# Blank matrix products and an early one-column gelu in the last image's back half

## What is computed

```python
out = softmax(q k^T * scale + rel_h + rel_w) @ v      # per window and head
x = shortcut + out @ proj_w + proj_b
y = layer_norm(x) * ln2_g + ln2_b
y = gelu(y @ fc1_w + fc1_b)                           # 192 -> 768, exact gelu
return x + (y @ fc2_w + fc2_b)                        # 768 -> 192
```

## Time and profile before

| | us |
|---|---|
| median of 3 runs | 534.57 |
| lowest, highest | 530.46, 537.25 |
| the profiled execution's own time | 535.51 |
| its span, first to last instruction | 533.7 |
| mean granted TensorE clock over the span | 0.965 |

### The profile page before, as it was taken

One profiled execution on the slowest core, in us unless ns is written; L12 is line 12 of the kernel. 1 busy time (PEld: TensorE's weight loads), 2 busy tenths in 40 slices (PEclk: granted clock), 3 DMA queues, 4 the chain that ended last, 5 costly groups with the idle time before them and its releaser, 6 DMA issues.

```text
span 533.7 us, 12298 instructions
## 1 busy us (share of the span) xinstructions
PE 508.3 (95%) x4544; PEld 463.4 (87%) x4544; DVE 390.2 (73%) x924; ACT 265.4 (50%) x526; POOL 135.9 (25%) x318
## 2 busy tenths in 40 slices
PE   7999889999999999999999999999999999998947
PEld 7999768899998999999998989999989899776737
DVE  5237887879888888879888888888887978764130
ACT  2112434565555565635545555646555555555602
POOL 1213222323122423223132324232232323220110
PEclk9669898999999999999999999999999999999978
DMA  6962232342404040401304040404031221303000
GB/s 170 250 164 76 68 105 86 98 120 58 133 16 143 2 143 3 134 12 52 93 17 129 2 144 2 142 3 129 16 111 34 74 72 33 113 2 93 0 16 15
DMA packets 29760, 40.98 MB, mean 77 GB/s; under 512 B 5796, under 2 KB 14468, under 8 KB 29700
## 3 DMA queue, kind: packets, MB, share of 16 engines
q1 hardware_dynamic: 29699, 40.20, 26.2%
HBM read 6.57 MB, written 1.57 MB: 15 GB/s over the span
## 4 chain that ended last, share of the span: by engine, by line
PE 89%; DVE 4%; issue 3%; ACT 3%; POOL 1%; DMA 0%; DVEq 0%; POOLq 0%; ACTq 0%
PE back L1250 17%; PE back L1469 12%; PE by_key L1409 9%; PE times_v L1419 9%; PE by_query L1394 9%; PE front_b L1250 8%; PE front_b L1362 6%; PE front_a L1362 6%; PE front_a L1250 4%; PE back L1435 2%; PE by_key L1286 2%; PE back L1442 1%; PE back L1298 1%; PE front_a L1298 1%; PE front_a L1371 1%
## 5 line engine op out<-in xcount | busy, mean ns | idle before, releaser
L1189 DVE TENSOR_REDUCE row_max<-by_query 128x2 f32<-128x512 f32 x186 | 127.7, 687 | 44.6 <-PE by_query L1394 43.4
L959 ACT ACTIVATE probs<-by_key 128x512 f32<-128x512 f32 x192 | 110.4, 596 | 76.6 <-PE by_key L1409 71.7
L1394 PE MATMUL by_query<-k_stack,q_stack 108*128 108x256 f32 x372 | 80.5, 298 | 2.4 <-DVE row_max L1189 2.3
L1409 PE MATMUL by_key<-q_stack,k_stack 110*128 110x256 f32 x384 | 80.4, 306 | 2.3 <-ACT probs L959 2.3
L1469 PE MATMUL back<-w,hid 128*128 128x192 f32 x384 | 69.6, 326 | 0.0
L1394 PEld LDWEIGHTS by_query<-k_stack,q_stack 108*128 108x128 f32 x372 | 57.5, 191 | 10.1 <-issue 6.6
L1409 PEld LDWEIGHTS by_key<-q_stack,k_stack 110*128 110x128 f32 x384 | 56.9, 190 | 10.3 <-issue 6.2
L1469 PEld LDWEIGHTS back<-w,hid 128*128 128x128 f32 x384 | 61.5, 190 | 0.3
L1250 PE MATMUL back<-xn_hi,w_hi 128*128 128x256 f32 x192 | 53.6, 290 | 1.9 <-DVE xn_hi L1098 1.6
L1250 PE MATMUL back<-xn_hi,w_lo 128*128 128x256 f32 x192 | 53.0, 287 | 0.0
L1419 PE MATMUL times_v<-probs,v_ones 128*32 128x256 f32 x768 | 52.3, 390 | 0.0
(11 more groups left out here) (138 smaller groups left out, 1000.2 us busy)
## 6 DMA issues: line engine op xcount, KB each, us to landing
q_stack<-q_hi SPq DMA_DIRECT2D x32, 192.0 KB, 2.7
k_stack<-k_hi SPq DMA_DIRECT2D x32, 192.0 KB, 3.1
q_stack<-rel_hi SPq DMA_DIRECT2D x32, 168.0 KB
q_stack<-rel_lo SPq DMA_DIRECT2D x32, 168.0 KB
q_stack<-q_lo SPq DMA_DIRECT2D x16, 192.0 KB, 3.0
k_stack<-k_lo SPq DMA_DIRECT2D x16, 192.0 KB, 3.1
X<-in_x SPq DMA_DIRECT2D x8, 192.0 KB, 7.2
k_stack<-av_t SPq DMA_DIRECT2D x8, 192.0 KB
```

The costliest lines, as they stand in the source:

```text
L959: act.activation(probs[h % NP], KB[h % 2][:, :].rearrange("p (k t) -> p k t", k=2), ACT.Exp).then_inc(s_ex, 1)
L1189: dve.tensor_reduce(row_max[:, h, :], scores(n, h)[:, :].rearrange("p (a t) -> p a t", a=TILES), AX, ALU.max).then_inc(s_smax, 1)
L1394: last = pe.matmul(scores(n, h)[:, a * TOK:(a + 1) * TOK], q_stack[n % 2][0:ROWS_Q, h, a * P:(a + 1) * P], k_stack[n % 2][0:ROWS_Q, h, :], ...
L1409: last = pe.matmul(KB[h % 2][:, c * TOK:(c + 1) * TOK], k_stack[n % 2][0:ROWS_K, h, c * P:(c + 1) * P], q_stack[n % 2][0:ROWS_K, h, :], st ...
```

## The change

A one-column tile `gelu_ready` is added. Behind `att_out` of the last image ACT applies gelu to one column of `blank`. On TensorE a new step-helper, `warm_drain(count)`, issues `count` products of `blank` with itself into `FA`; for the last image it stands ahead of the waits of `att_transposes` (6 products), `projection` (2), `transpose1` (14) and `fc1`'s part 0 (6). Nothing reads what these write.

```diff
         blank = sb("blank", [P, P])
+        gelu_ready = sb("gelu_ready", [P, 1])
...
                 act.activation(att_t[:, :, :], BB[:, 0:512].rearrange("p (c t) -> p c t", c=2), ACT.Copy).then_inc(s_ato, 1)
+                if n == N2 - 1:
+                    act.wait_ge(s_blank, 1)
+                    act.activation(gelu_ready[:, :], blank[:, 0:1], ACT.Gelu)
...
+            def warm_drain(count):
+                pe.wait_ge(s_psub, N2)
+                for _ in range(count):
+                    pe.matmul(FA[:, 0:P], blank[:, :], blank[:, :], start=True, stop=True)
...
             def transpose1(n, part):
+                if n == N2 - 1:
+                    warm_drain(14)
                 pe.wait_ge(n_hat[1], n + 1)
...
             def att_transposes(n, part):
+                if n == N2 - 1:
+                    warm_drain(6)
                 pe.wait_ge(s_att, n + 1)
...
             def projection(n, part):
                 l = n // IMAGES
+                if n == N2 - 1:
+                    warm_drain(2)
                 pe.wait_ge(s_ato, n + 1)
...
             def fc1(n, part):
                 l = n // IMAGES
                 if part == 0:
+                    if n == N2 - 1:
+                        warm_drain(6)
                     pe.wait_ge(n_lo[1], n + 1)
```

## The result

| | before | after |
|---|---|---|
| median of 21 runs, us | 534.57 | 530.69 |
| lowest, highest | 530.46, 539.62 | 527.29, 535.72 |
| span of the profiled execution | 533.7 | 526.4 |
| mean granted clock over the span | 0.965 | 0.987 |

The ratio after to before is 0.9932, with a 95% interval of 0.9910 to 0.9955: 3.6 us less, between 2.4 and 4.8. The ratio leaves out executions over 1.5% above the fastest of the same kernel, which the medians include. The forecast was 530.4.

A forecast was written before the change was run, and what follows sets the result against it. TensorE was taken as the bound over the whole run, with gains only where it waits in the tail. 1.4 + 0.45 + 2.4 - 0.1 = 4.15 us off the median 534.57 gave 530.4, own range 527.5 to 533.

The forecast's parts named there:

- projection at full clock: In the tail, the projection's eight records take 1.47 us instead of 2.94 at full clock; 1.4 us gained.
- four transposes: Ahead of fc1 in the tail, they take 0.67 us at full clock instead of 1.12; 0.45 us gained.
- fc1 and the table load: From fc1's first product to fc2, thirty products run through without the load between: 3.65 us for 6.06, 2.4 gained.
- blanks late before `att_transposes`: Before `att_transposes`, 1.33 us of blanks in 1.36 of room; 0.1 us charged for a slower first record.
- The clock stays up: In the tail, blanks in PE's waits hold the granted clock at 1.00 from 505 to fc2's end.
- Room for the blanks: In four PE waits, full-clock blanks of 1.33, 0.44, 3.11, 1.33 us against room of 1.36, 0.84, 3.4, 1.7.
- The load's price: Between fc1 and the first gelu, the load costs 1.28 us without drain; by the skill page at most 1.4 more.
- third rival: At `high1`, the copy after the early gelu asks for its own table; 1.65 us gained, 532.9; chance 0.05.
- The first rival: In the tail of other executions, less clock was lost; only 1.2 us gained at the load, 533.4; chance 0.14.
- a change ahead of 505: Before the tail, where nothing was edited: a difference there would make the prediction wrong; no size given.
- The second rival: Before `transpose1` and `fc1`, half-clock blanks overrun by 2.8 and 0.95 us; 3.4 slower, 538.0; chance 0.08.
- The fourth: In the tail, blanks do not count for the clock, which falls as before; 0.3 us gained, 534.3; chance 0.09.

## Why the prediction was right

The forecast held by its own steps:

| step | forecast | measured |
|---|---|---|
| projection at full clock | 1.4 | 2.94 - 1.58 = 1.36 |
| four transposes | 0.45 | 1.12 - 0.67 = 0.45 |
| fc1 and the table load | 2.4 | 6.22 - 3.92 = 2.30 |
| blanks late before `att_transposes` | -0.1 | 0.0 |
| sum | 4.15 | 4.11 |

- *The clock stays up*: yes, 1.00 in all of the tail. That it hangs on the blanks and not on the gelu is shown by the two runs with one part each (20.11 and 22.34). In all, the clock was 1.00 from the copy of the last `times_v` to the end of fc2 in the eight profiles with blanks in all four places, and fell in the four where some or all were missing.
- *fc1 with the load taken together*: the order of ends came out as worked out. The gelus of the first two blocks ended before PE had done its second ten, and the 30 products run as one. The gain was 0.1 smaller than forecast: by the start of fc2's first record in PE's timeline, as the forecast counted, it took 6.06 before and 3.76 after, where 3.65 was forecast (the chain counts 0.16 more in both). The forecast has one slow record in the 30; there are two, the first of each group that has a wait of its own: 0.23 to the next at the head and 0.20 once within, in place of 0.12.
- *Room for the blanks*: 12, 4, 28 and 12 records fit. The tightest place, 1.36 us for 1.33, was the one in the chain, at no cost. With doubled counts the overrun came out as the same arithmetic has it.
- *The load's price*: 1.28 with nothing behind it (508.46 to 509.75 with the gelu). The drain of about 1380 ns in the Trainium skill, "ScalarE: Activation LUTs", section "What ACT_TABLE_LOAD costs", does not show; the load's part measured 1.26, not 2.66. No load stands at L907, between the gelus, so the third rival falls. That agrees with what the same page of the Trainium skill says in "Table sets: the hidden batching unit", that copy is in every set.
- *The first rival*, that other executions had less to regain, finds no support in the granted clock over the span, which is on record for every execution: on average 0.965 in 35 of the kernel before and 0.978 in the change's 21; 0.966 in 12 with the early gelu alone, 0.976 in 12 with the blanks alone. With two levels, the time at half clock is 2 x (1 - clock) x span: an estimate of 37 us before and 23 after. That is 14 less, where the profiled tail had 3.2 and 6.7 at half; from which part of the span the average comes isn't shown. The average gain by the ratio is 3.6 (2.4 to 4.8), and the 4.1 of the profiled tail lies within it.
- *The number* came closer than it could be known. The forecast started from the median of three runs, and the median of 21, spread over 9.2 us, happens to be the same 534.57. The profiled span was forecast at 529.5 and measured 526.4; the difference is a change ahead of 505, one of the prediction's own signs of being wrong. It is smaller than the 5.1 by which two executions of the changed program differ there (504.59, 509.72), so it says nothing of the edit. What moves the start of the tail so far is open.
- *The second rival* is real where the first blanks are missing, and needs the clock down at `transpose1`. Its price of 2.8 was too high, as the clock came back while the blanks ran: 1.28 measured. *The fourth* falls with it.
- What I took "less surely", that blanks raise a lowered clock, stays unsure: it rose under them in the run without the front blanks, with products at half clock right ahead. Why 16 records at 24.80 to 28.50 did not lift it is open.

## What to carry to other kernels

Where a chain of dependent steps is the last thing a core does, TensorE's clock can fall in the waits or just behind them, and the price is paid in the products that follow; independent products placed in the waits held it here, where they fit at full clock with the clock up on entry, and half of what fits did in one profile. A table load can be had early with one column of a dead tile, and is worth its whole length only where the engine that waits has nothing of its own to do meanwhile (1.26 of 1.28 here; about 0.5 where PE had products at half clock). Judge a change of under one per cent by the edited stretch in the profile, not by the span.

## What the runs showed of the hardware that was not expected

- With the clock at 1.00 and all blanks fitting, the tail is the same to 0.04 us (18.81 to 18.85 in six profiles of four programs), while the time at which it starts ranged from 504.59 to 511.23 in these six; the change alone showed 504.59 and 509.72.
- The clock can fall in a wait or behind it: it fell at 511.1, within 0.69 us of idle time (the kernel before), but was 1.00 through a wait of 3.27 us without products, and fell while the next blanks ran (the run without the 14).
- The clock went from 0.50 to 1.00 while products of zeros were all that PE ran, about 2.85 us behind their start and behind 2.93 us of the projection's products at 0.50 (the run without the 6 and 2).
